# Two feed-forward steps from the middle into self-attention, and a new order of the rest of the middle's steps, in a hosted transformer kernel

## The chip, the cores and the metric

One Trainium2 chip, one core. The metric is the device time of one execution in microseconds; the kernel before has a median of 3263.27 us over 3 runs (3256.77 to 3267.13).

## What is computed

```python
x = xattn0(x, ctx, ctx, 2 * fside)        # 16 heads of 64, 1024 queries, 64 keys, float32; then a layernorm
h1 = ln(x);  x = attn(h1, h1) + x         # self-attention: 16 heads of 32, q, k, v and softmax weights in 8 bits
h2 = ln(x);  x = attn(h2, ctx) + x        # cross-attention: 64 keys, 8 bits
h3 = ln(x)
a, g = split(h3 @ ff_w1 + ff_b1)          # 512 -> 2 x 2048
x = (a * gelu(g)) @ ff_w2 + ff_b2 + x     # 2048 -> 512
```

x has 4 batches of 1024 tokens with 512 features. The projections and the feed-forward are float32 and are computed as three products of high and low parts (hi hi, hi lo, lo hi).

## The kernel before

The 4096 tokens are 8 chunks of 512, two per batch. For each batch the kernel runs `cross` (first attention, layernorm, q, k, v) of both chunks, then for each chunk `self_attention` and `middle` (output projection o1, layernorm h2, q2, cross-attention, o2, layernorm h3). In names such as chunk n, steps have the form kind, group, part: g3.2 is part 2 of group 3.

**The feed-forward of a chunk has no stage of its own.** It is cut into 48 steps, in the order g0 a0 g1 d0 a1 g2 d1 a2 g3 d2 a3 d3, four steps to each. A g step is 128 rows of the gate's half of ff_w1, an a step (the gated rows) 128 rows of the other half, a d step 128 tokens of the product with ff_w2. A step is four quarters of three 128x512 matmuls (L1827, L1828, L1829) into PSUM bank 6 or 7 in turn. The later chunk's stages are the host: at each of their slots every engine calls its own `feed` with the same plan, and that gives the quarters or steps that are due. Behind the matmuls of a g step ScalarE copies the bank with the bias into `gate` (L1283), and after the fourth it runs Gelu over all of `gate` (L1289). Behind an a step VectorE multiplies into `gate` (L1614), ScalarE rounds to u_hi (L1275), GpSimd takes u_lo (L1051). Behind a d step VectorE adds to x (L1537). A d step's matmuls wait for u_lo of its group's last a step. These followers come with a lag in slots: copies, products and additions one slot later, u_hi and u_lo up to two and three slots later in self-attention and one slot later elsewhere.

**Plans** (`host_quarters`, L73). Even chunks use FROM_S: 28 steps in the self-attention of the next chunk and 20 in its middle. Chunks 1, 3 and 5 use FROM_A: 16 steps in the two `cross` stages of the next batch, 18 in the self-attention of its first chunk, 14 in that chunk's middle. Their hosts are chunks 2, 4 and 6. The last chunk stands alone at the end. Within the self-attention the quarters are spread evenly over the 70 slots before the last; in the middle a list of slots says where each step goes.

**Self-attention** has 64 units (head and 128 queries) and 71 slots. In slot s TensorE computes the scores of unit s (L2111, L2112), then the guest's quarters, then the transpose of unit s-5 (L2123), and in half of the slots a part of the weighted values a1 (L2137). VectorE takes the scores out with the row's minimum (L1712) and the transposed weights (L1725), ScalarE takes the exponential (L1353), GpSimd the denominator and the rounding (L1024, L1026, L1031), and once, near slot 10, the bias of o1 (L945). When a head group's a1 is complete, ScalarE's `weighted_high` writes ht_hi (L1224) and the whole back (L1225), and VectorE's `weighted_low` ht_lo (L1439). For the last group both calls stand behind the loop over the slots:

```python
for s in range(S_SLOTS):
    ...
    if n >= 1:
        feed(n - 1, host_plan(n - 1), first_in_S(n) + s)
weighted_high(n, HG - 1)
```

**The middle** has 23 slots. On TensorE, each with the guest's step ahead of it: slots 0 to 3 o1 of four tiles of 128 tokens, 2 to 5 the transposes of h2, 6 to 9 q2, 10 to 13 the scores s2.0 to s2.3 (L2183), 13 to 16 the transposes p2T of the weights (L2191), 14 to 17 the weighted values a2 (L2200), 15 to 18 o2, 19 to 22 the transposes of h3. VectorE does, for each tile of the cross-attention, row maximum, subtraction, row sum and reciprocal (L1761, L1764, L1768 to L1772) and w2T (L1777), GpSimd the scaling and w2b (L1092, L1097). p2T uses one bank, so each transpose waits for w2T of the one before.

**Queues.** SP issues all loads in program order: for a step that is the last user of a piece of ff weights it waits for the step and loads the next piece into the same slot of a ring of three. q2's weights are loaded behind the self-attention's steps, o2's at slot 4 of the middle, the turned queries of the next chunk at slot 12.

Of the kernel before, what the change touches and what calls it, by code (L numbers as in the profile page):

```python
# [72 lines left out]
def host_quarters(in_A, in_S, m_slots):  # L73

    ends = []
    for c in range(NC if in_A else 0):
        for s in range(A_SLOTS):
            ends.append(4 * in_A * c + (4 if s < A_TAIL else (12, 19, 26, 32)[min(s - A_TAIL, 3)]))
    first, start = 4 * NC * in_A, len(ends)
    for s in range(S_SLOTS):  # L80
        ends.append(min(first + 4 * in_S, first + 4 * in_S * (s + 1) // (S_SLOTS - 1)))
    for s in range(M_SLOTS):
        ends.append(first + 4 * in_S + 4 * sum(1 for m in m_slots if m <= s))
    assert ends[-1] == 4 * NF
    return Plan(ends, range(start, start + S_SLOTS))
# [1 line left out]


FROM_S = host_quarters(0, 28, [s for s in range(M_SLOTS) if s not in (16, 21, 22)])
FROM_A = host_quarters(8, 18, (0, 1, 2, 3, 4, 6, 10, 11, 12, 13, 15, 17, 19, 21))  # L90
ALONE = Plan([4 * (k + 1) for k in range(NF)])


def begins_in_A(n):
    return n % NC == NC - 1 and n < CHUNKS - 1


def host_plan(n):
    return FROM_A if begins_in_A(n) else FROM_S

# [163 lines left out]
def build(nc, a, out):  # L264

    ctx = ExitStack()
    with ctx:
# [303 lines left out]
        def _(sp):  # L571
# [139 lines left out]
            def feed(n, plan, i):  # L711

                if n == 0:
                    for v in pieces_due(plan, LAG_KEEP, i):
                        keep_piece(v)
                for k in steps_ending(plan, i):
                    for v in range(PIECES):
                        after = PIECE_NEXT.get((n, v))
                        if PIECE_END[v] == k and after is not None:
                            if not (begins_in_A(after[0]) and after[1] in (0, 8, 9)):  # L720
                                load_piece(*after)
# [50 lines left out]
            def cross(n):  # L772
# [28 lines left out]
                else:  # L801
                    for s in range(A_SLOTS):
                        feed(NC * b - 1, FROM_A, A_SLOTS * c + s)
                if c == 0:
# [85 lines left out]
        def _(pool):  # L890
# [72 lines left out]
            def cross(n):  # L963

                def host(s):
                    if n >= NC:
                        feed(NC * (n // NC) - 1, FROM_A, A_SLOTS * (n % NC) + s)

# [72 lines left out]
            def feed(n, plan, i):  # L1041

                if n == 0:
                    for v in pieces_due(plan, LAG_LOW, i):
                        if v % 2 == 0:
                            piece_low(v)
                for k in steps_due(plan, LAG_LOW, i):
                    kind, j, m = F_STEPS[k]
                    if kind == "a":
                        pool.wait_ge(u_hi_done.sem, u_hi_done.at((n, j, m)))  # L1050
                        pool.tensor_tensor(u_lo[:, m, :], gate[:, m, :], u_hi[:, m, :].bitcast(F32), ALU.subtract  # L1051
                                           ).then_inc(u_lo_done.sem, 1)
# [69 lines left out]
        def _(act):  # L1122
# [141 lines left out]
            def feed(n, plan, i):  # L1264

                if n == 0:
                    for v in pieces_due(plan, LAG_HIGH, i):
                        piece_high(v)
                for k in steps_due(plan, LAG_HIGH, i):
                    kind, j, m = F_STEPS[k]  # L1270
                    if kind == "a":
                        if m == 0 and (j > 0 or n > 0):
                            wait_filled(act, ("f", n if j else n - 1, F_AT["d", j - 1 if j else 3, 3]))
                        wait_emptied(act, ("f", n, k))
                        act.activation(u_hi[:, m, :], gate[:, m, :], ACT.Copy).then_inc(u_hi_done.sem, 1)  # L1275
                for k in steps_due(plan, 1, i):
                    kind, j, m = F_STEPS[k]
                    if kind == "g":
                        key = ("f", n, k)
                        wait_filled(act, key)  # L1280
                        if j > 0 or n > 0:
                            act.wait_ge(u_lo_done.sem, u_lo_done.at((n, j - 1, m) if j else (n - 1, 3, m)))
                        act.activation(gate[:, m, :], bank(bank_of(key)), ACT.Identity,  # L1283
                                       bias=cols["L1_xattn_ff_b1"][:, FT + 4 * j + m:FT + 4 * j + m + 1]
                                       ).then_inc(emptied[bank_of(key)], 1)
                        if m == 3:
                            wait_emptied(act, ("f", n, k - 1))
                            wait_emptied(act, key)
                            act.activation(gate[:], gate[:], ACT.Gelu).then_inc(gelu_done.sem, 1)  # L1289

            def cross(n):

                def host(s):
                    if n >= NC:
                        feed(NC * (n // NC) - 1, FROM_A, A_SLOTS * (n % NC) + s)

# [112 lines left out]
        def _(dve):  # L1409
# [192 lines left out]
            def feed(n, plan, i):  # L1602

                if n == 0:
                    for v in pieces_due(plan, LAG_LOW, i):
                        if v % 2 == 1:
                            piece_low(v)
                for k in steps_due(plan, 1, i):
                    kind, j, m = F_STEPS[k]
                    key = ("f", n, k)  # L1610
                    if kind == "a":
                        dve.wait_ge(gelu_done.sem, gelu_done.at((n, j)))
                        wait_filled(dve, key)
                        emptied_bank(dve.scalar_tensor_tensor(gate[:, m, :], bank(bank_of(key)),  # L1614
                                                              cols["L1_xattn_ff_b1"][:, 4 * j + m:4 * j + m + 1],
                                                              gate[:, m, :], ALU.add, ALU.mult), key)
                    if kind == "d":
                        if j == 0 and m == 0:
                            dve.wait_ge(bias_added.sem, bias_added.at(("ff_b2", n)))
                        residual(key, xs(n, m))  # L1620

            def cross(n):

                def host(s):
                    if n >= NC:
                        feed(NC * (n // NC) - 1, FROM_A, A_SLOTS * (n % NC) + s)

# [180 lines left out]
        def _(pe):  # L1808
# [187 lines left out]
            def feed(n, plan, i):  # L1996

                for quarter in range(plan.ends[i - 1] if i else 0, plan.ends[i]):
                    step_k, k = divmod(quarter, KT)
                    kind, j, m = F_STEPS[step_k]  # L2000
                    key = ("f", n, step_k)
                    o = bank(bank_of(key))
                    if k == 0:
                        wait_empty(key)
                    v = 2 * (step_k // 4)
                    if kind == "d":
                        v += k // 2
                        if m == 0 and k % 2 == 0:
                            wait_piece(pe, n, v)
                        if m == 0 and k == 0:  # L2010
                            pe.wait_ge(u_lo_done.sem, u_lo_done.at((n, j, 3)))
                        r = PIECE_SLOT[n, v]
                        w = [t[r][:].rearrange("p (k n) -> p k n", n=512)[:, k % 2, :] for t in (fw_hi, fw_lo)]
                        ts = slice(m * P, m * P + P)
                        ins = three(o, u_hi[:, k, ts], u_lo[:, k, ts], w[0], w[1], k == 0, k == KT - 1)
                    else:
                        v += m // 2
                        if m % 2 == 0 and k == 0:
                            wait_piece(pe, n, v)
                        if step_k == 0:  # L2020
                            wait_emptied(pe, ("h3T", n, k))
                        r = PIECE_SLOT[n, v]
                        cs = slice(m % 2 * P, m % 2 * P + P)
                        w = [t[r][:].rearrange("p (k n) -> p k n", n=256)[:, k, cs] for t in (fw_hi, fw_lo)]
                        ins = three(o, w[0], w[1], h3_hi[:, k, :], h3_lo[:, k, :], k == 0, k == KT - 1)
                    if k == KT - 1:
                        done(ins, key)
# [8 lines left out]
            def cross(n):  # L2036

                def host(s):
                    if n >= NC:
                        feed(NC * (n // NC) - 1, FROM_A, A_SLOTS * (n % NC) + s)  # L2040

# [210 lines left out]
```

## Time and profile before

| what | us |
|---|---|
| median of 3 runs | 3263.27 |
| the profiled execution, its own time | 3261.57 |
| its span | 3259.8 |
| TensorE busy | 2903.8 (89%) |
| VectorE busy | 2125.2 (65%) |
| ScalarE busy | 1517.4 (47%) |
| GpSimd busy | 1763.0 (54%) |
| mean granted clock of TensorE | 0.94 |
| first to last scores, self-attention of chunks 2, 4, 6 | 131.0, 133.5, 132.9 |
| from there to the next self-attention | 106.9, 106.9, 107.6 |

Times in rows count from the start of the span. PE is TensorE's matmuls, PEld its weight loads, DVE VectorE, ACT ScalarE, POOL GpSimd. A matmul's duration contains its way through the array; matmuls follow each other faster than that. The clock is a share of full speed.

### The profile page before, as it was taken

What the parts mean: (1) busy time and instruction counts of PE and PEld (TensorE: products, weight loads), DVE (VectorE), ACT (ScalarE), POOL (GpSimd) and SP (SyncE); (2) the same over time, 40 slices, a digit from 0 to 9 for tenths busy, and PEclk for the clock granted to TensorE, in tenths of its full rate; (3) what the DMA queues carried; (4) which work ended last, traced back from release to release, by engine and by line L of the source; (5) the groups of instructions that cost most, each with busy time, mean ns of one, the idle gap of its engine ahead of it and who ended that gap; (6) DMA issues with size and microseconds to landing.
All of it is one profiled execution on the core that took longest, in us unless ns stands there. A gap on an engine that the chain in (4) does not pass through costs nothing.

```text
span 3259.8 us, 50933 instructions
## 1 busy us (share of the span) xinstructions
PE 2903.8 (89%) x19712; PEld 2124.7 (65%) x19712; DVE 2125.2 (65%) x3539; ACT 1517.4 (47%) x2258; POOL 1763.0 (54%) x1750
## 2 busy tenths in 40 slices
PE   7677786998799899899899999899989999899998
PEld 6566455566577657667677656666767756666777
DVE  4456686884755596796665497687564588688521
ACT  5343552773333464474333464375333366276321
POOL 3556583883546284585455186386364277377321
PEclk9889657999899999999999999899999989999999
DMA  8754103335443313324443313323453322232444
GB/s 272 246 191 158 59 1 126 133 117 206 150 171 125 118 66 130 136 92 168 147 168 117 126 53 130 128 105 138 147 184 103 149 79 97 92 143 85 174 166 157
DMA packets 199760, 436.42 MB, mean 134 GB/s; under 512 B 94944, under 2 KB 103392, under 8 KB 182368
## 3 DMA queue, kind: packets, MB, share of 16 engines
q1 hardware_dynamic: 199520, 433.15, 37.6%
q8 instruction: 158, 2.59, 0.3%
q14 instruction: 82, 0.67, 0.1%
HBM read 363.38 MB, written 65.54 MB: 132 GB/s over the span
## 4 chain that ended last, share of the span: by engine, by line
PE 59%; POOL 15%; DVE 12%; issue 5%; ACT 5%; DMA 3%; SPq 1%; POOLq 0%; DVEq 0%; ACTq 0%
PE psum L1827 17%; PE psum L1828 16%; PE psum L1829 16%; POOL w1b L1031 6%; PE psum L2123 4%; DVE e L1712 2%; PE psum L2111 2%; POOL rec L1026 2%; PE psum L2137 1%; POOL u_lo L1051 1%; DMA fw_lo<-pieces 1%; DMA unsplit<-in_L_xattn_ff_w 1%; POOL x L945 1%; POOL w_lo L925 1%; DVE w1T L1725 1%
## 5 line engine op out<-in xcount | busy, mean ns | idle before, releaser
L1353 ACT ACTIVATE e<-e,nb 128x1024 f32<-128x1024 f32 x512 | 588.2, 1149 | 331.2 <-DVE e L1712 328.0
L1712 DVE TENSOR_SCALAR_CACHE_REDUCE e<-psum,nscale 128x1024 f32<-128x1024 f32 x512 | 653.0, 1277 | 66.6 <-POOL w1b L1031 44.0
L1031 POOL TENSOR_SCALAR w1b<-e,rec 128x1024 f16<-128x1024 f32 x512 | 578.3, 1130 | 98.5 <-POOL rec L1026 57.3
L1827 PE MATMUL psum<-h_hi,fw_hi 128*128 128x512 f32 x1024 | 460.3, 450 | 44.9 <-DVE h_lo L1439 14.9
L1828 PE MATMUL psum<-h_lo,fw_hi 128*128 128x512 f32 x1024 | 413.4, 404 | 0.0
L1725 DVE TENSOR_SCALAR w1T<-psum 128x1024 bf16<-128x1024 f16 x512 | 352.2, 688 | 93.0 <-PE psum L2123 90.0
L1829 PE MATMUL psum<-h_hi,fw_lo 128*128 128x512 f32 x1024 | 412.4, 403 | 0.0
L2123 PEld LDWEIGHTS psum<-ident,w1b 128*128 128x128 f16 x4096 | 254.2, 103 | 239.9 <-issue 133.9
L2123 PE MATMUL psum<-ident,w1b 128*128 128x128 f16 x4096 | 345.0, 232 | 72.3 <-POOL w1b L1031 40.1
L1827 PEld LDWEIGHTS psum<-h_hi,fw_hi 128*128 128x128 f32 x1024 | 197.5, 193 | 164.8 <-issue 99.6
L1051 POOL TENSOR_TENSOR u_lo<-gate,u_hi 128x512 fp32r<-128x512 f32 x128 | 164.5, 1286 | 225.6 <-ACT u_hi L1275 219.4
L1537 DVE TENSOR_TENSOR x<-psum,x 128x512 f32<-128x512 f32 x192 | 130.7, 685 | 225.6 <-PE psum L1829 225.3
L1827 PE MATMUL psum<-w_hi,ht_hi 128*128 128x512 f32 x640 | 257.5, 402 | 20.1 <-DVE e L1640 13.7
L925 POOL TENSOR_TENSOR w_lo<-mixed,w_hi 128x512 fp32r<-128x512 f32 x140 | 190.1, 1380 | 132.8 <-ACT w_hi L1232 132.8
L1829 PE MATMUL psum<-w_hi,ht_lo 128*128 128x512 f32 x640 | 251.6, 393 | 0.0
L1828 PE MATMUL psum<-w_lo,ht_hi 128*128 128x512 f32 x640 | 251.4, 393 | 0.0
L1827 PE MATMUL psum<-fw_hi,u_hi 128*128 128x512 f32 x512 | 219.7, 429 | 31.5 <-POOL u_lo L1051 14.7
L1024 POOL TENSOR_SCALAR den<-sum,delta 128x2 f32<-128x2 f32 x256 | 75.9, 297 | 285.7 <-ACT e L1353 269.4
L1829 PEld LDWEIGHTS psum<-h_hi,fw_lo 128*128 128x128 f32 x1024 | 199.1, 194 | 46.3
L1170 ACT ACTIVATE qt<-psum,rounder,inv 128x512 f32<-128x512 f32 x128 | 99.9, 780 | 259.1 <-PE psum L1829 256.2
L1828 PEld LDWEIGHTS psum<-h_lo,fw_hi 128*128 128x128 f32 x1024 | 200.0, 195 | 25.3
L2112 PE MATMUL psum<-k_odd,q_turned 32*128 32x512 bf16 x512 | 214.7, 420 | 0.0
(197 smaller groups left out, 6076.1 us busy)
## 6 DMA issues: line engine op xcount, KB each, us to landing
fw_hi<-pieces SPq DMA_DIRECT2D x168, 512.0 KB, 3.3
fw_lo<-pieces SPq DMA_DIRECT2D x168, 512.0 KB, 4.3
w_hi<-kept SPq DMA_DIRECT2D x45, 1024.0 KB, 4.9
w_lo<-kept SPq DMA_DIRECT2D x45, 1024.0 KB, 7.8
mixed<-mixed SPq DMA_DIRECT2D x32, 1024.0 KB, 5.3
fbias<-in_fside_Bx16xSxS SPq DMA_DIRECT2D x64, 256.0 KB, 3.0
unsplit<-in_L_xattn_ff_w SPq DMA_DIRECT2D x24, 512.0 KB, 5.0
pieces<-fw_hi SPq DMA_DIRECT2D x24, 512.0 KB, 2.6
```

What stands on the lines that cost most here:

```text
L925: pool.tensor_tensor(w_lo[s][:, k, :], w_mixed[s][:, k, :], w_hi[s][:, k, :].bitcast(F32), ALU.subtract).then_inc(block_lo_done.sem, 1)
L1031: pool.tensor_scalar(w1b[u % NH][:], e1[u % NE][:], rec1[:, u % 8:u % 8 + 1], HALF, ALU.mult, ALU.add).then_inc(w1_ready.sem, 1)
L1051: pool.tensor_tensor(u_lo[:, m, :], gate[:, m, :], u_hi[:, m, :].bitcast(F32), ALU.subtract).then_inc(u_lo_done.sem, 1)
L1353: act.activation(e1[s % NE][:], e1[s % NE][:], ACT.Exp, bias=nb1[:, s % NE:s % NE + 1], scale=-1.0, accum_out=sum1[:, s % 8:s % 8 + 1]).th ...
L1537: return emptied_bank(dve.tensor_tensor(xt, bank(bank_of(key)), xt, ALU.add), key)
L1712: emptied_bank(dve.tensor_scalar(e1[s % NE][:], psum[:, i:i + 2, :].rearrange("p i n -> p (i n)"), nscale[:, 0:1], LARGEST, ALU.mult, ALU.min,
L1725: emptied_bank(dve.tensor_scalar(w1T[u % 8][:].rearrange("p k q -> p (k q)"), bank(bank_of(key)).bitcast(FP16), -HALF, W_HIGH, ALU.add, AL ...
L1827: pe.matmul(o, s_hi, m_hi, start=first, stop=False)
L1828: pe.matmul(o, s_hi, m_lo, start=False, stop=False)
L1829: return pe.matmul(o, s_lo, m_hi, start=False, stop=last)
L2112: ins = pe.matmul(bank(i + 1), q1_turned[turned, hg, t * P:t * P + P], k1[1][turned, hg, :], start=True, stop=True)
L2123: ins = pe.transpose(bank(bank_of(key)).bitcast(FP16)[:, k * P:k * P + P], w1b[u % NH][:, k * P:k * P + P], ident16[:])
```

## The change

One line, the plan of chunks 1, 3 and 5.

```diff
-FROM_A = host_quarters(8, 18, (0, 1, 2, 3, 4, 6, 10, 11, 12, 13, 15, 17, 19, 21))
+FROM_A = host_quarters(8, 20, (1, 2, 3, 4, 6, 11, 12, 14, 17, 19, 20, 21))
```

The steps' order stays. Self-attention gets steps 16 to 35 instead of 16 to 33, that is g3.2 and g3.3 as well, so 80 quarters instead of 72. The middle's steps by slot:

| | before | after |
|---|---|---|
| g3.2, g3.3 | 0, 1 | (self-attention) |
| d2.0 to d2.3 | 2, 3, 4, 6 | 1, 2, 3, 4 |
| a3.0 to a3.3 | 10, 11, 12, 13 | 6, 11, 12, 14 |
| d3.0 to d3.3 | 15, 17, 19, 21 | 17, 19, 20, 21 |

In self-attention the slots with two quarters are 34 and 69 before, and 6, 13, 20, 27, 34, 41, 48, 55, 62 and 69 after. The copy of a group's fourth g step and its Gelu come one slot behind it: for g3 in slot 2 of the middle before, in slot 70 of self-attention after.

## Rows read from the trace of the kernel before

**Rows 1.** Busy time by stretch: self-attention of chunks 2 and 3, middle of chunk 2.
```profile
core 0: us, PE busy (x) PEld busy (x) DVE busy (x) ACT busy (x) POOL busy (x), PEclk, DMA share, GB/s
1116.10:1247.10 131.00, 119.82 (x1230) 71.31 (x1230) 120.77 (x198) 90.76 (x145) 109.12 (x127) 0.97 0.20 73
1354.00:1496.80 142.80, 140.43 (x1339) 90.72 (x1338) 127.87 (x205) 104.77 (x162) 112.97 (x130) 0.99 0.37 134
...
1247.10:1354.00 106.90, 95.81 (x570) 74.76 (x562) 62.16 (x105) 30.84 (x41) 40.36 (x33) 0.95 0.32 114
```

**Rows 2.** Timeline of TensorE around the softmax of chunk 2's middle.
```profile
start us, us, engine line op out<-in xcount [idle before <-releaser]
1314.67 0.61 PE L2191 MATMUL psum<-ident,w2b 128*128 128x128 f16 x8
1321.43 1.01 PE L2191 MATMUL psum<-ident,w2b 128*128 128x128 f16 x8 [6.15 <-DVE w2T L1777]
...
1325.58 0.76 PE L1827 MATMUL psum<-fw_hi,u_hi 128*128 128x512 f32 x1 [2.58 <-POOL u_lo L1051]
...
1330.44 0.62 PE L2191 MATMUL psum<-ident,w2b 128*128 128x128 f16 x8
```

**Rows 3.** The same view, slot 10: q2.3's last matmul, a3.0's first, s2.0.
```profile
1299.77 0.39 PE L1829 MATMUL psum<-ht_hi,w_lo 128*128 128x512 f32 x1
1299.99 0.39 PE L1827 MATMUL psum<-h_hi,fw_hi 128*128 128x512 f32 x1
...
1302.71 0.61 PE L2183 MATMUL psum<-k,q2T 128*128 128x256 bf16 x4
```

**Rows 4.** Busy time by stretch: slots 21 to 63 of chunks 2 and 3.
```profile
1161.50:1247.40 85.90, 80.34 (x899) 48.69 (x898) 82.73 (x136) 63.16 (x101) 72.92 (x88) 1.00 0.17 63
1402.90:1497.30 94.40, 94.33 (x970) 61.52 (x969) 85.40 (x138) 67.14 (x105) 76.43 (x91) 1.00 0.26 91
```

**Rows 5.** The same for L1827 alone, one matmul to a quarter.
```profile
core 0: us, PE busy (x) PEld busy (x), PEclk, DMA share, GB/s
1161.50:1247.40 85.90, 20.88 (x42) 7.82 (x42) 1.00 0.17 63
1402.90:1497.30 94.40, 30.12 (x66) 12.29 (x66) 1.00 0.26 91
```

**Rows 6.** Two gaps of TensorE (timeline), and busy time by stretch behind their starts.
```profile
1143.75 1.04 PE L2123 MATMUL psum<-ident,w1b 128*128 128x128 f16 x8 [4.34 <-POOL w1b L1031]
...
1142.20:1149.10 6.90, 5.35 (x55) 3.33 (x55) 3.88 (x6) 3.00 (x5) 6.00 (x8) 0.51 0.00 0
...
789.25 0.79 PE L1827 MATMUL psum<-h_hi,fw_hi 128*128 128x512 f32 x1 [4.84 <-ACT gate L1283]
...
787.30:794.10 6.80, 4.85 (x11) 3.80 (x12) 1.95 (x3) 2.88 (x4) 0.00 (x0) 0.50 0.38 154
```

**Rows 7.** Timeline of ScalarE, end of chunk 2's self-attention and slots 1 and 2.
```profile
1258.62 0.69 ACT L1283 ACTIVATE gate<-psum,col_L_xattn_ff_b 128x512 f32<-128x512 f32 x1 [4.74 <-PE psum L1829]
1259.21 0.68 ACT L1224 ACTIVATE ht_hi<-psum,unit_v 128x512 fp32r<-128x512 f32 x1
...
1267.59 0.69 ACT L1283 ACTIVATE gate<-psum,col_L_xattn_ff_b 128x512 f32<-128x512 f32 x1 [4.75 <-PE psum L1829]
1268.35 1.28 ACT L1289 ACT_TABLE_LOAD   x1
1269.64 1.92 ACT L1289 ACTIVATE gate<-gate 128x2048 f32<-128x2048 f32 x1
```

**Rows 8.** Timeline of VectorE in the same place.
```profile
1260.47 0.69 DVE L1439 TENSOR_TENSOR ht_lo<-psum,ht_hi 128x512 fp32r<-128x512 f32 x1 [2.60 <-ACT psum L1225]
```

**Rows 9.** Timeline of TensorE in the same place: last of a1, first of o1.
```profile
1258.52 0.63 PE L2137 MATMUL psum<-w1T,v 128*32 128x128 bf16 x32
...
1261.94 0.39 PE L1827 MATMUL psum<-w_hi,ht_hi 128*128 128x512 f32 x1
```

**Rows 10.** Timeline of TensorE, s2.0 of chunk 0, which hosts nothing.
```profile
533.17 0.60 PE L2183 MATMUL psum<-k,q2T 128*128 128x256 bf16 x4 [1.71 <-issue]
```

**Rows 11.** Timeline of VectorE in chunk 2's softmax.
```profile
1321.20 0.73 DVE L1614 SCALAR_TENSOR_TENSOR gate<-psum,col_L_xattn_ff_b,gate 128x512 f32<-128x512 f32 x1
...
1324.32 0.63 DVE L1777 TENSOR_SCALAR w2T<-psum 128x1024 bf16<-128x1024 f16 x1
```

**Rows 12.** Timeline of GpSimd in chunk 2's softmax.
```profile
1323.04 1.05 POOL L1097 TENSOR_SCALAR w2b<-e 128x1024 f16<-128x1024 f32 x1 [0.22 <-POOL e L1092]
1324.17 1.27 POOL L1051 TENSOR_TENSOR u_lo<-gate,u_hi 128x512 fp32r<-128x512 f32 x1
```

## The prediction

> **What bounds the kernel now.** I read first the table of stages. In self-attention that hosts an odd chunk (chunk 2's) VectorE is busy for 120.8 of 131.0 us; where it hosts an even one (chunk 3's, 28 steps) TensorE is, 140.4 of 142.8 [rows 1]. So the first has room on TensorE. The middle is TensorE's: 95.8 of 106.9 us [rows 1]. Then I read what TensorE waits for inside chunk 2's middle; it repeats in the middles of chunks 4 and 6, so each price below counts three times. It has one hole, in the softmax of the cross-attention: behind the first transpose it idles 6.15 us for VectorE, and a little later 2.58 us for u_lo of a3.3 [rows 2].
>
> **Part 1: two steps, g3.2 and g3.3, go into self-attention.** A step is 12 matmuls, a quarter 3 of them. At full clock they follow each other by 0.227 us (12 from 1299.99 to 1302.71 [rows 3]), so a quarter is 0.68 us, a step 2.72. The plan gives one quarter to each of the 70 slots and a second where it rounds up: before in slots 34 and 69, now in 6, 13, 20 and so on to 69, eight more. The moved steps bring VectorE nothing, ScalarE two 0.69 us gate copies and Gelu.
>
> What does a quarter cost there? From slot 21 to 63 the two kinds of stage show 85.9 us with 42 quarters and 94.4 us with 66 [rows 4, 5]: 0.35 us per quarter along that line. TensorE is saturated at its upper end (94.3 of 94.4), VectorE nearly at its lower (82.7 of 85.9), so the first quarters are cheaper: I take 0.25 for the five that fall there, 1.2 us. The three before slot 21 meet a stage that is filling or at half clock (after the 4.34 us for which TensorE waits for GpSimd, busy with the bias, the clock is at 0.51 for 6.9 us [rows 6]); I take 0.8. Sum **+2.0**; bounds 0 (all in TensorE's slack) and 8 x 0.68 = 5.4. The gate copies hide in ScalarE's idle time, 40 of 131 us. SP's loads of the pieces move up with their steps; each piece has the slot of a ring of three and a step now takes 131/20 = 6.6 us against 7.3, so no load gets late. GpSimd's and VectorE's work of a1, d1 and a2 keeps its count and comes earlier.
>
> **Part 2: the end of self-attention.** Here I see the main cost. g3.1 ends the stage's quarters now; its copy runs at 1258.62, and right behind it on ScalarE comes ht_hi of the last head group at 1259.21 [rows 7]. From there VectorE's ht_lo starts 1.26 us later, at 1260.47 [rows 8], and o1's first product follows, at 1261.94, hidden behind g3.2 (TensorE ends a1 at about 1258.9 and is busy all along [rows 9]). With the change g3.3 is the step whose copy stands there, and `feed` adds the whole gate's Gelu behind it, in slot 70, ahead of `weighted_high(n, 3)`, which stands after the loop. From the start of that copy to the end of Gelu it is 3.97 us in the old place: 1267.59, a table load of 1.28, Gelu of 1.92 until 1271.56 [rows 7]. So Gelu ends at 1258.62 + 3.97 = 1262.6, ht_hi follows, ht_lo starts 1.26 later and ends 0.69 later: 1264.5, and o1 starts at 1264.6. Nothing covers it, since slot 0 of the middle is now empty. Against 1261.94 that is **+2.7**, with g3.2's 2.72 us of matmuls already gone from in front of o1. Bounds: -0.6 if ht_hi were not delayed (ht_lo ends 1261.16 now), +3.3 if o1's handover were slow.
>
> The Trainium skill, page "ScalarE: Activation LUTs", section "What ACT_TABLE_LOAD costs", puts a switch of sets at 1283 ns and 1380 ns of drain. The load agrees; this trace shows no drain (0.08 us idle before the load, Gelu 0.01 after it [rows 7]). By the page the term would be 4.1 instead of 2.7, an estimate.
>
> **Part 3: the clock behind that gap.** TensorE would stand from 1258.9 to 1264.6, 5.7 us. The nearest rows: 4.34 us of idle time, then 6.9 us at 0.51; 4.84 us, then 6.8 us at 0.50 [rows 6]. Both are the level of 1.2 GHz, and begin 3.3 us into the gap. Taken over: half clock from 1262.2 to 1269.1, of which 4.5 us hold work, half of it lost: **+2.2** (bounds 0 and 3.4).
>
> **Part 4: slots 1 to 10 of the middle.** d2.0 to d2.3 each take the place of another step, and a3.0 goes from slot 10 to slot 6, where d2.3 was. There its gate product and its u_hi lie ahead of the quantisations of q2.1, in idle time of VectorE and ScalarE, and u_lo in GpSimd's. Slot 10 loses 2.72 us, but q2's last rounding, which a3.0 covered, is bare: in chunk 0, with no guest, s2.0 waits 1.71 us [rows 10]. q2.3's last matmul, at 1299.77 for 0.39, then gives s2.0 at 1301.9 instead of 1302.71 [rows 3]: **-0.9** (bounds 0 and -2.7).
>
> **Part 5: the softmax hole.** From s2.0 on VectorE has no gap; the pace of s2.1 and s2.2 is the same, since a3.1 and a3.2 stay. a3.3 goes from slot 13 to 14, behind the first transpose, and fills part of the 6.15 us. Its gate product (0.73, at 1321.20) leaves the chain ahead of the last sum, so w2T.1 ends at about 1324.3 instead of 1324.95 [rows 11]. d3.0, which waits for u_lo of 1324.17 + 1.27 = 1325.44, moves from slot 15 to 17, and the third transpose, w2b being ready at 1324.09, can go at 1324.45 instead of TensorE's standing until 1325.58 [rows 2, 12]: **-1.1** (bounds 0 and -2.0). What follows to the end of the middle is the same list of products in another order, dense before, and three steps behind o2.3 instead of two cover its norm. Half clock cost d3.0 4.86 us instead of 2.72 here (1325.58 to 1330.44 [rows 2]), 2.1 too much. Two or three gaps of under 4 us take the place of the long one; I count **-0.5** (bounds -2.1 and +2.1). If that cover is gone, o2's products are what half clock hits.
>
> Sum for one pair: 2.0 + 2.7 + 2.2 - 0.9 - 1.1 - 0.5 = 4.4 us; three times 13.2. The profiled execution took 3261.57 us (span 3259.8, 1.8 around it) and comes to 3274.8; the median of the three runs is 1.7 above it, so I forecast 3276.5.
>
> **Rivals.** A measurement of this kernel can tell about 0.3%, 9.8 us, from no change.
>
> *Wash.* Self-attention takes the quarters at nothing, and TensorE stays at full clock over the new gap: 0 + 2.7 + 0 - 0.9 - 1.1 - 0.5 = 0.2 a pair, 3264. For it: VectorE's 92% in [rows 1]. Against: both gaps in [rows 6] were shorter and brought half clock. With one of the two terms alone it is 3270 to 3271, still within 0.3%. Chance 0.36.
>
> *Faster: the clock.* The mechanism is half clock that goes away: a fuller self-attention keeps TensorE at full clock behind GpSimd's bias (6.9 us at 0.51 [rows 6], 3.4 us back), and the refilled hole does the same for o2 (2.1). With the quarters free and the new gap at full clock: -3.4 + 2.7 - 0.9 - 1.1 - 2.1 = -4.8 a pair, 3249. It decides if GpSimd's bias no longer starves TensorE for over 4 us; against it, that wait is for w1b, which more quarters don't bring earlier. Chance 0.10.
>
> *Slower still: quarters at full price.* Each second quarter of a slot stalls VectorE and is never regained, 5.4 instead of 2.0, and half clock stays through the broken hole: 5.4 + 2.7 + 3.4 - 0.9 - 1.1 + 1.5 = 11.0 a pair, 3296. For it: the line through [rows 4, 5] is already half of the full price. Chance 0.10.
>
> *The switch with a drain.* If ScalarE needed some more time between the copy and the load, 1.4 us as a bound, that is 4.2 us in all, 3281. The copy and the load stand 0.07 us apart [rows 7]. The drain of the page named above, in the Trainium skill, would be such a time. Chance 0.04.
>
> *The change doesn't do what it says.* The plan is read in the code: quarters 64 to 143 in the 70 slots, so this has no chance worth a number.
>
> The forecast case has 0.40. Range: from 3256, two thirds of the way from no change to the faster rival, to 3289, where the terms' upper bounds begin to add up. Faster 0.10, same 0.36, slower 0.54 (0.40 + 0.10 + 0.04).
>
> **What would show it.** In the profile after, at the end of self-attention of chunks 2, 4 and 6: a table load and Gelu directly ahead of ht_hi, ht_lo 3.3 us later against a1's end, and o1's first product after 5 to 6 us of idle time with VectorE's ht_lo as releaser, then half clock. The self-attention itself 133 us instead of 131. s2.0 released by q2T. The hole in pieces of 4, 4 and under 2 us, d3.0 behind o2.1. I am wrong if ht_hi does not stand behind Gelu, if the clock holds over the gap, or if the stage from slot 21 to 63 grows by over 3 us or not at all.

## The result and the profile after

The changed kernel takes 3281.83 us (median of 5 runs, 3278.30 to 3287.16) against 3264.19 (5 runs): ratio 1.0057, 95% interval 1.0045 to 1.0069. It is 0.57% slower; 17.6 us lie between the medians, 13.2 were forecast. Executions in a slower state are left out of every ratio here and below, and the one trace of `e2_cover` is of such an execution and is not read.

The profiled execution has a span of 3283.0 us, 23.2 more than before. To see where, I cut each trace at the same instructions: the first scores of each self-attention, its last scores, the last matmul of a1, the first of o1, the first scores s2.0 of the cross-attention and the first matmul of the third transpose p2T.2 (L2191). Start to start, in us, for the three chunks that host an odd one. A pair is such a chunk's self-attention and middle together; half clock means a granted clock of 0.50, the level of 1.2 GHz.

| from, to | before: chunks 2, 4, 6 | after: chunks 2, 4, 6 | mean change | forecast |
|---|---|---|---|---|
| first to last scores | 131.0, 133.6, 132.9 | 134.6, 138.0, 134.8 | +3.3 | +2.0 |
| to the end of a1 | 11.8, 11.8, 12.1 | 12.3, 12.3, 12.3 | +0.4 | 0 |
| to o1 | 3.02, 3.04, 3.04 | 5.77, 5.77, 5.78 | +2.7 | +2.7 |
| to s2.0 | 40.8, 40.7, 40.7 | 42.9, 42.6, 41.4 | +1.5 | +1.3 (2.2 - 0.9) |
| to p2T.2 | 27.7, 27.7, 28.1 | 21.4, 21.4, 21.4 | -6.4 | |
| to the next self-attention | 23.6, 23.6, 23.6 | 27.8, 29.2, 28.5 | +4.9 | -1.6 with the row above |
| the whole pair | 237.9, 240.4, 240.5 | 244.8, 249.3, 244.2 | +6.5 | +4.4 |

d3.0 has changed sides of the cut at p2T.2, so those two rows go together: -1.5. Three pairs make 19.5 us, close to the 17.6 of the medians. The other 3.7 us of this profile are what is left of larger differences in stages that the change leaves alone: 4.5 us more ahead of chunk 0's first scores, 3.9 more from there to chunk 1's (221.7 before, 225.6 after), 1.6 more from there to chunk 2's, and 5.6 less from chunk 5's first scores to chunk 6's (513.3 before, 507.6 after). More on this at the end.

The end of chunk 2's self-attention, ScalarE, timeline after; it answers to [rows 7]:

```profile
start us, us, engine line op out<-in xcount [idle before <-releaser]
1272.72 0.69 ACT L1283 ACTIVATE gate<-psum,col_L_xattn_ff_b 128x512 f32<-128x512 f32 x1 [4.73 <-PE psum L1829]
1273.48 1.28 ACT L1289 ACT_TABLE_LOAD   x1
1274.78 1.91 ACT L1289 ACTIVATE gate<-gate 128x2048 f32<-128x2048 f32 x1
1276.59 0.67 ACT L1224 ACTIVATE ht_hi<-psum,unit_v 128x512 fp32r<-128x512 f32 x1
```

VectorE and TensorE in the same place, answering to [rows 8, 9]:

```profile
1277.85 0.69 DVE L1439 TENSOR_TENSOR ht_lo<-psum,ht_hi 128x512 fp32r<-128x512 f32 x1 [5.88 <-ACT psum L1225]
...
1272.61 0.63 PE L2137 MATMUL psum<-w1T,v 128*32 128x128 bf16 x32
1278.80 0.77 PE L1827 MATMUL psum<-w_hi,ht_hi 128*128 128x512 f32 x1 [5.55 <-DVE ht_lo L1439]
```

Gelu stands between the copy and ht_hi, 3.97 us from the start of the copy to its end as in its old place, and o1 waits 5.55 us for ht_lo, behind the chain copy, table load, Gelu, ht_hi. Busy time by stretch after; the clock is the last column but two:

```profile
core 0: us, PE busy (x) PEld busy (x) DVE busy (x) ACT busy (x) POOL busy (x), PEclk, DMA share, GB/s
1278.10:1285.00 6.90, 6.20 (x15) 4.94 (x16) 1.07 (x2) 0.00 (x0) 0.00 (x0) 0.51 0.63 252
...
1126.20:1260.70 134.50, 126.00 (x1254) 76.71 (x1254) 121.66 (x199) 91.88 (x148) 109.61 (x128) 0.96 0.21 79
1260.70:1370.90 110.20, 93.27 (x546) 72.72 (x538) 61.53 (x104) 29.26 (x39) 40.42 (x32) 0.94 0.28 101
...
1173.00:1262.00 89.00, 85.18 (x917) 52.83 (x915) 83.71 (x138) 63.87 (x101) 72.94 (x89) 0.98 0.20 72
```

The gap is followed by 6.9 us at half clock. The two stages answer to [rows 1]. The last row is slots 21 to 63, 89.0 us where [rows 4] have 85.9; VectorE is idle for 5.3 us of it instead of 3.2.

The softmax of chunk 2's middle, TensorE, timeline after, answering to [rows 2, 10]:

```profile
1321.69 0.60 PE L2183 MATMUL psum<-k,q2T 128*128 128x256 bf16 x4 [1.71 <-issue]
...
1333.09 1.03 PE L2191 MATMUL psum<-ident,w2b 128*128 128x128 f16 x8 [3.94 <-POOL w2b L1097]
1333.88 0.78 PE L1827 MATMUL psum<-h_hi,fw_hi 128*128 128x512 f32 x1
...
1340.39 0.61 PE L2191 MATMUL psum<-ident,w2b 128*128 128x128 f16 x8 [2.46 <-DVE w2T L1777]
...
1343.10 1.03 PE L2191 MATMUL psum<-ident,w2b 128*128 128x128 f16 x8 [1.76 <-POOL w2b L1097]
1344.07 0.64 PE L2200 MATMUL psum<-w2T,v 128*64 128x128 bf16 x8
1344.63 0.80 PE L1827 MATMUL psum<-w_hi,ht_hi 128*128 128x512 f32 x1
```

s2.0 waits the 1.71 us of [rows 10] to the hundredth. The one hole is now three idle times of 3.94, 2.46 and 1.76 us with a3.3 in between, and p2T.2 goes 21.4 us behind s2.0.

What I had not priced is in the middle of self-attention, where g2's Gelu stands in slot 28. ScalarE, GpSimd, VectorE and TensorE behind it, timelines after:

```profile
1190.01 1.28 ACT L1289 ACT_TABLE_LOAD   x1
1191.30 1.92 ACT L1289 ACTIVATE gate<-gate 128x2048 f32<-128x2048 f32 x1
1193.24 1.28 ACT L1353 ACT_TABLE_LOAD   x1
1194.53 1.15 ACT L1353 ACTIVATE e<-e,nb 128x1024 f32<-128x1024 f32 x1
...
1195.87 0.29 POOL L1024 TENSOR_SCALAR den<-sum,delta 128x2 f32<-128x2 f32 x1 [3.41 <-ACT e L1353]
...
1198.41 1.28 DVE L1712 TENSOR_SCALAR_CACHE_REDUCE e<-psum,nscale 128x1024 f32<-128x1024 f32 x1 [1.74 <-POOL w1b L1031]
1203.29 0.69 DVE L1725 TENSOR_SCALAR w1T<-psum 128x1024 bf16<-128x1024 f16 x1 [1.78 <-PE psum L2123]
...
1198.35 0.62 PE L2123 MATMUL psum<-ident,w1b 128*128 128x128 f16 x8 [1.90 <-POOL w1b L1031]
1199.56 0.75 PE L1827 MATMUL psum<-fw_hi,u_hi 128*128 128x512 f32 x1
...
1199.60:1203.00 3.40, 3.40 (x15) 2.50 (x14) 1.91 (x5) 2.48 (x4) 3.00 (x4) 0.50 0.00 0
```

While ScalarE has Gelu in place of exponentials, GpSimd runs dry for 3.41 us, VectorE for 1.74, TensorE for 1.90. Then the clock is at half for 3.4 us, and in it lie the six matmuls of slot 34, one of those with two quarters: VectorE waits again, 1.78 us. In the kernel before, with this Gelu in slot 32, the same three waits are 2.60, 1.05 and 1.21 us, and the clock holds.

Cut at VectorE's first instruction of slots 21, 42 and 63, slots 21 to 41 take 43.9 to 44.1 us before and 45.9 after, slots 42 to 62 take 42.0 and 43.1. How much of the first is the clock can be read from `e7_high_cover`, a run below that has the same quarters in self-attention as the changed kernel. Its slots 21 to 41 in chunks 2 and 6, where only the first has half clock behind Gelu:

```profile
1175.50:1221.40 45.90, 43.28 (x458) 26.80 (x457) 41.68 (x69) 34.11 (x53) 35.87 (x45) 0.96 0.14 48
2670.30:2714.60 44.30, 41.65 (x458) 25.83 (x458) 41.65 (x70) 34.06 (x52) 35.54 (x45) 1.00 0.15 51
```

VectorE's first wait is 1.74 us in both. So at full clock the two more quarters of these slots cost 0.2 us, and the half clock costs 1.6. Of the 12 such stages in the traces of the changed kernel, `e1_high_first`, `e3_move_only` and `e7_high_cover`, 11 have that half clock and take 45.8 or 45.9 us.

### The profile page after: what moved, and what is told of

It is laid out like the page before. It is cut to its first block, busy times and chain, and to the rows that moved or that the text cites. A ratio compares the mean times of both kernels' runs of the same rounds, so it can differ in the third digit from the quotient of the medians.

```text
span 3283.0 us, 50933 instructions
## 1 busy us (share of the span) xinstructions
PE 2915.3 (89%) x19712; PEld 2136.9 (65%) x19712; DVE 2122.1 (65%) x3539; ACT 1517.3 (46%) x2258; POOL 1759.0 (54%) x1750
## 4 chain that ended last, share of the span: by engine, by line
PE 61%; DVE 12%; POOL 11%; issue 5%; ACT 5%; DMA 3%; SPq 1%; POOLq 0%; DVEq 0%; ACTq 0%
PE psum L1827 18%; PE psum L1828 16%; PE psum L1829 16%; PE psum L2123 5%; POOL w1b L1031 4%; PE psum L2111 3%; DVE e L1712 3%; PE psum L2137 2%; POOL rec L1026 1%; DMA unsplit<-in_L_xattn_ff_w 1%; DVE w1T L1725 1%; POOL x L945 1%; DMA fw_lo<-pieces 1%; POOL w_lo L925 1%; DVE e L1764 1%
## 5 line engine op out<-in xcount | busy, mean ns | idle before, releaser
L1827 PE MATMUL psum<-h_hi,fw_hi 128*128 128x512 f32 x1024 | 461.1, 450 | 41.5 <-DVE h_lo L1439 14.9
L1827 PEld LDWEIGHTS psum<-h_hi,fw_hi 128*128 128x128 f32 x1024 | 197.8, 193 | 160.0 <-issue 98.7
L1827 PE MATMUL psum<-w_hi,ht_hi 128*128 128x512 f32 x640 | 263.5, 412 | 36.8 <-DVE ht_lo L1439 19.2
L1537 DVE TENSOR_TENSOR x<-psum,x 128x512 f32<-128x512 f32 x192 | 130.9, 686 | 243.2 <-PE psum L1829 243.2
L1827 PE MATMUL psum<-fw_hi,u_hi 128*128 128x512 f32 x512 | 218.4, 427 | 22.1 <-POOL u_lo L1051 7.0
```

Source lines behind the costliest of these rows:

```text
L1537: return emptied_bank(dve.tensor_tensor(xt, bank(bank_of(key)), xt, ALU.add), key)
L1827: pe.matmul(o, s_hi, m_hi, start=first, stop=False)
```

## The experiments

Theory A is the prediction's: Gelu ahead of ht_hi holds up o1, and half clock follows. Rival B: the quarters in self-attention are the cost. Rival C: the new order of the middle is a loss of its own. The runs of a group below were compared with the kernel before on the same chip, which had medians of 3263.03, 3263.32 and 3264.20 us in the three groups. Stage times are from each run's trace, cut as above.

**ht_hi ahead of Gelu** (`e1_high_first`), on the changed kernel:

```diff
+                    if s == S_SLOTS - 1:
+                        weighted_high(n, HG - 1)
                     if n >= 1:
                         feed(n - 1, host_plan(n - 1), first_in_S(n) + s)
-                weighted_high(n, HG - 1)
```

> The changed kernel with one difference: in the last slot of self-attention ScalarE writes ht_hi of the last head group before the guest's gate copy and Gelu, not behind them. Theory A (Gelu ahead of ht_hi holds up o1, and the gap brings half clock): TensorE's gap ahead of o1 falls from 5.77 us to about 2.5, the half clock behind it (3.4 to 6.8 us) goes; 3.3 + about 2.5 us for each of three pairs, so about 3264 us instead of 3281.8. Rival B (the eight more quarters in self-attention are what costs, the gap is hidden by something later): not more than 4 us come back, 3278 or above.

Measured: 3269.05 us, ratio 1.0015 (1.0004 to 1.0026). Timelines of ScalarE and TensorE in this run (from L1363 on lines are one higher):

```profile
1265.78 0.69 ACT L1224 ACTIVATE ht_hi<-psum,unit_v 128x512 fp32r<-128x512 f32 x1 [5.28 <-PE psum L2138]
1266.36 0.65 ACT L1225 ACTIVATE psum<-psum,unit_v 128x512 f32<-128x512 f32 x1
1266.93 0.69 ACT L1283 ACTIVATE gate<-psum,col_L_xattn_ff_b 128x512 f32<-128x512 f32 x1
1267.69 1.28 ACT L1289 ACT_TABLE_LOAD   x1
...
1268.00 0.47 PE L1828 MATMUL psum<-w_hi,ht_hi 128*128 128x512 f32 x1 [2.27 <-DVE ht_lo L1440]
```

From a1's last matmul to o1's first it is 2.49 us in all three chunks, 2.27 of it idle, no half clock follows, and from o1 to s2.0 it is 40.0 us each time. The pairs take 240.1, 240.1 and 239.9: 6.1 less than the changed kernel's mean. That two calls of ScalarE in another order bring back some 13 of the 17.6 us shows theory A, though the total stays 5 us above the 3264 that I expected. By stage the cure is worth 3.3 us ahead of o1 and 2.3 behind it, and 0.6 of that is lost again between s2.0 and the next self-attention: 5.0 a pair. The other 1.1 of the 6.1 lie in self-attention, which the edit does not touch: in the changed kernel's profile chunk 4 has 13.7 us of half clock near its start, and 138.0 us where the other two have 134.6 and 134.8. In this run the self-attention keeps its 134.7. The edit acts in the odd chunks too; their stretches show no shift that all traces with it share.

**d2.0 in slot 0** (`e2_cover`), on the changed kernel:

```diff
-FROM_A = host_quarters(8, 20, (1, 2, 3, 4, 6, 11, 12, 14, 17, 19, 20, 21))
+FROM_A = host_quarters(8, 20, (0, 2, 3, 4, 6, 11, 12, 14, 17, 19, 20, 21))
```

> The changed kernel with d2.0 in slot 0 of the middle instead of slot 1, so that its matmuls stand in the gap ahead of o1. Theory A: o1 starts when it did (ht_lo sets it), the gap is 2.7 us of matmuls and about 3.1 us idle, and slot 1 loses a step: 2.7 us and perhaps 1.5 to 3 us of half clock for each pair, 3265 to 3270 us. Rival B (the middle's length is set elsewhere, by the softmax of the cross-attention): under 3 us in all, 3279 or above.

Measured: 3265.17 us, ratio 1.0012 (1.0001 to 1.0023), as theory A has it, at the lower end of its range. Only its times are used: that o1 still starts when it did, with Gelu ahead of ht_hi, and how much half clock is left, was not seen. What d2.0 in slot 0 does by stage can be read only together with the other cure, in `e7_high_cover` below.

**The quarters moved, the middle's order old** (`e3_move_only`), on the changed kernel:

```diff
-FROM_A = host_quarters(8, 20, (1, 2, 3, 4, 6, 11, 12, 14, 17, 19, 20, 21))
+FROM_A = host_quarters(8, 20, (2, 3, 4, 6, 10, 11, 12, 13, 15, 17, 19, 21))
```

> 20 steps in self-attention as in the changed kernel, but the middle's twelve steps in their old slots (2, 3, 4, 6, 10 to 13, 15, 17, 19, 21). Theory A says the new order is a gain of 0.9 (slot 10), 1.5 (softmax) and 0.6 us (behind it) for each pair, so this is 9 us slower than the changed kernel, about 3291. Rival C (the new order of the middle is itself a loss): it is faster than the changed kernel, 3275 or below.

Measured: 3276.76 us, ratio 1.0038 (1.0025 to 1.0051), between the two, but 5 us below the changed kernel, where 9 above were forecast. My 3291 was a fault of reckoning: I counted the 0.9 us of slot 10 as a gain of the order. It is the sum of a step that leaves (-2.7, in this run too) and of the bare rounding of q2 (+1.9), and only the second belongs to the order. So the order's share is +1.9 in slot 10 against -1.5 in softmax and behind: about nothing. From o1 to the next self-attention this run takes 91.7, 92.0 and 91.7 us, the changed kernel 92.1, 93.2 and 91.3; of the 1.8 us a pair by which this run's profile is shorter, 1.4 lie in self-attention, where the plan is the same.

**The order alone** (`e4_order_only`), 18 steps in self-attention:

```diff
-FROM_A = host_quarters(8, 18, (0, 1, 2, 3, 4, 6, 10, 11, 12, 13, 15, 17, 19, 21))
+FROM_A = host_quarters(8, 18, (0, 0, 1, 2, 3, 4, 6, 11, 12, 14, 17, 19, 20, 21))
```

> 18 steps in self-attention as before; the middle has g3.2 and g3.3 both in slot 0 and the other twelve in the changed kernel's slots. Theory A: Gelu comes in slot 1, behind ht_hi, no gap ahead of o1; the middle gains 1.5 + 0.6 in the softmax and loses 1.8 where q2's rounding is bare: 0 to -1 us for each pair, 3261 to 3265 us. Rival C (the new order is a loss): above 3270.

Measured: 3264.28 us, ratio 1.0006 (0.9998 to 1.0015); pairs of 237.8, 240.1 and 237.9 us, 1.0 below before on the mean. Rival C falls: the order as a whole costs nothing that can be seen here, and brings nothing either. Self-attention is 130.9, 132.8 and 131.1 here and 134.3, 134.5 and 134.3 in the run above: the eight quarters cost 2.8 us there and 0.6 in the tail to a1's end (12.3 against 11.7), and the order has no part in it.

**The second quarters away from Gelu** (`e5_doubles_away`), on the changed kernel. `host_quarters` takes a list of the slots with two quarters:

```diff
+        if doubles:
+            ends.append(min(first + 4 * in_S, first + s + 1 + sum(1 for d in doubles if d <= s)))
...
-FROM_A = host_quarters(8, 20, (1, 2, 3, 4, 6, 11, 12, 14, 17, 19, 20, 21))
+FROM_A = host_quarters(8, 20, (1, 2, 3, 4, 6, 11, 12, 14, 17, 19, 20, 21),
+                       doubles=(6, 9, 13, 20, 38, 45, 48, 55, 62, 69))
```

> The changed kernel with the slots of two quarters at 6, 9, 13, 20, 38, 45, 48, 55, 62, 69: Gelu of g2 stays in slot 28 of self-attention, but slots 27 and 34 next to it have one quarter. Theory D (a second quarter right ahead of and behind Gelu is what stalls VectorE: 1.74 and 1.78 us of idle time in slots 32 and 34, and 3.4 us of half clock): slots 21 to 41 take about 44 us instead of 46.0, self-attention of chunks 2 and 6 132.5 instead of 134.7, about 3275 us in all. Rival E (each more quarter costs its share of TensorE's time wherever it stands): 134.5 as before, 3280.

Measured: 3280.62 us (4 executions), ratio 1.0053 (1.0039 to 1.0067), not told from the changed kernel, and by the total what rival E has. The stage speaks for theory D only in part. Between the first instructions of VectorE in slots 21 and 42, chunk 2 takes 44.7 us and chunks 4 and 6 43.5, the changed kernel 45.9, and self-attention of chunks 4 and 6 is 132.2 and 132.3. But chunk 2's is 135.3, with 10.2 us of half clock in its first slots and 3.4 behind Gelu, where chunks 4 and 6 have neither. So what moving the two quarters changed is the second stall (under 0.8 us now) and, in two chunks of three, the half clock; the whole gained too little to show. The first stall behind Gelu stays what it was, so the quarters beside it are not its cause; VectorE, chunk 6 (in this run and the next, lines behind the plan are four higher):

```profile
2696.18 1.28 DVE L1716 TENSOR_SCALAR_CACHE_REDUCE e<-psum,nscale 128x1024 f32<-128x1024 f32 x1 [1.81 <-POOL w1b L1035]
```

**Gelu in slot 29** (`e6_gelu_slot_29`), one entry of that list moved:

```diff
-                       doubles=(6, 9, 13, 20, 38, 45, 48, 55, 62, 69))
+                       doubles=(6, 13, 20, 38, 45, 48, 52, 55, 62, 69))
```

> As the run with doubles away, with one double moved from slot 9 to slot 52, so that Gelu of g2 comes in slot 29. GpSimd takes units in pairs and waits for the odd one's exponential, so behind slot 29 it has a pair left to work on while ScalarE is away. Theory F (this pairing matters): VectorE's idle time behind Gelu falls under 1.5 us and the stage is 1 us shorter than with doubles away, 3272. Rival: the same within 0.5 us a stage, 3275.

Measured: 3271.47 us, ratio 1.0024 (1.0012 to 1.0036), the total of theory F. VectorE behind Gelu, chunk 2:

```profile
1197.49 1.28 DVE L1716 TENSOR_SCALAR_CACHE_REDUCE e<-psum,nscale 128x1024 f32<-128x1024 f32 x1 [1.12 <-POOL w1b L1035]
```

The stall is 1.12 us instead of 1.81; slots 21 to 41 take 42.7 us in each of the three chunks, and no half clock follows Gelu in any of them. With slots 42 to 62 (43.0) that makes 85.7 us with six slots of two quarters; the changed kernel has 89.0 with as many, the kernel before 86.1 with one. So there the five more quarters of slots 21 to 62 cost nothing, in these slots and with this Gelu. The stage as a whole is not 1 us shorter, as theory F has it: first to last scores are 133.6, 133.5 and 131.8 us, 133.0 on the mean against 133.3 with doubles away, since slots 0 to 20 of chunks 2 and 4 have 10.2 us of half clock at their start. The rest of the gain is in the tail behind the last scores, 11.6 instead of 12.3, and 0.9 a pair behind o1's start, which no theory had named. That the pairing of units in `scale_unit` shortens the stall fits the trace but was not varied by itself; the kernel before has a stall of 1.05 us with Gelu in slot 32, an even slot like 28, so the pairing alone does not say where it is short.

**Both cures of the gap** (`e7_high_cover`): the edits of `e1_high_first` and `e2_cover` together.

> The changed kernel with both cures: ht_hi ahead of Gelu, and d2.0 in slot 0 of the middle. Theory A: no gap ahead of o1 (3.0 us from a1's last matmul to o1's first, as before), 40.0 - 2.7 = 37.3 us from there to the scores of the cross-attention, so 2.2 us for each pair below the run with ht_hi first: 3262 us, level with the kernel before, because what is left is self-attention's 2 to 3 us. Rival: the gap of 2.5 us that it closes was hidden, 3268.

Measured: 3259.65 us, ratio 0.9988 (0.9979 to 0.9997). From a1 to o1 it is 3.02 to 3.04 us, from there to s2.0 37.2, a pair 237.1 on the mean, 2.9 below `e1_high_first`. With 20 steps in self-attention the kernel is now level with the one before or slightly faster, so the loss of the move goes with an end of self-attention that fits it. It is no gain yet: the next run gets as far with the middle's order alone.

**Only the softmax's order** (`e8_softmax_order`), on the kernel before:

```diff
-FROM_A = host_quarters(8, 18, (0, 1, 2, 3, 4, 6, 10, 11, 12, 13, 15, 17, 19, 21))
+FROM_A = host_quarters(8, 18, (0, 1, 2, 3, 4, 6, 10, 11, 12, 14, 17, 19, 20, 21))
```

> The kernel before (18 steps in self-attention, 14 in the middle) with only a3.3 moved from slot 13 to 14 and d3.0 to d3.3 from 15, 17, 19, 21 to 17, 19, 20, 21. Theory A: the softmax gains 1.5 us and what follows it 0.6, and a3.0 still covers q2's rounding in slot 10, so 2.1 us for each pair: about 3257 us. Rival C (the new order gives nothing, since half clock comes back in the broken hole): 3263.

Measured: 3260.19 us, ratio 0.9984 (0.9975 to 0.9993), pairs of 237.1, 236.7 and 239.2, 1.9 below before on the mean. So this half of the change is a gain by itself, but of less than I gave it, and less than the pairs say: from s2.0 to the next self-attention, the only part that the edit touches, it is 1.05 us shorter on the mean (50.4 against 51.5) where 2.1 were forecast. The other 0.9 lie in self-attention and its tail. Half clock did come back in the broken hole, as rival C has it: 13.7, 13.7 and 10.2 us in the three chunks against 10.2 each before. But the gains are 1.0, 1.1 and 1.1 us, so its return is not seen to have cost anything. TensorE in chunk 2's softmax:

```profile
1316.98 1.03 PE L2191 MATMUL psum<-ident,w2b 128*128 128x128 f16 x8 [3.66 <-POOL w2b L1097]
...
1324.30 0.61 PE L2191 MATMUL psum<-ident,w2b 128*128 128x128 f16 x8 [1.42 <-DVE w2T L1777]
...
1327.01 1.03 PE L2191 MATMUL psum<-ident,w2b 128*128 128x128 f16 x8 [1.76 <-POOL w2b L1097]
```

**All three** (`e9_all_three`): `e7_high_cover` with the quarters of `e6_gelu_slot_29`.

> The run with both cures of the gap (ht_hi ahead of Gelu, d2.0 in slot 0) with the quarters of the run that has Gelu in slot 29 (second quarters in 6, 13, 20, 38, 45, 48, 52, 55, 62, 69). If the three findings add up, a pair takes 237.1 us less 1.7 in self-attention (134.6 to about 133.0) and 0.7 in its tail (12.3 to 11.6), 234.7 us: 7 us below the run with both cures, about 3253 us, and 0.3% below the kernel before. If they don't (the stage before only shifts work into half clock), 3259.

Measured: 3253.38 us, ratio 0.9972 (0.9955 to 0.9988). Busy time by stretch, the two stages of chunk 2:

```profile
1116.60:1248.80 132.20, 125.57 (x1256) 76.22 (x1256) 121.77 (x199) 92.28 (x148) 110.66 (x128) 0.96 0.21 80
1248.80:1350.60 101.80, 91.28 (x544) 71.15 (x540) 61.61 (x105) 28.75 (x39) 39.81 (x32) 0.95 0.30 109
```

The pairs take 234.0, 236.1 and 234.0, 234.7 on the mean, which was forecast: the findings add up. (The profiled execution, at 3244.98 us, was one of the shortest; the forecast is compared with the median.)

**Second quarters in the tail** (`e10_tail_doubles`): there, slots 55 and 62 for 65 and 67.

> As the run with all three, but the second quarters of slots 55 and 62 moved to 65 and 67, behind the last scores, where TensorE idles 0.5 to 1.0 us in each slot. Theory G (TensorE's idle time of the tail takes them): self-attention 1 us shorter, tail longer by under 0.5, 0.5 us a pair, 3251. Rival: the tail is a chain through GpSimd and TensorE and grows by the 1.4 us that they cost, 3254.

Measured: 3253.09 us, ratio 0.9968 (0.9956 to 0.9981), level with the last, though the traced pairs are 1.0 us longer on the mean. The tail grows from 11.7 to 13.0 us, by what the two quarters cost, as the rival has it; self-attention is 132.3 instead of 132.7. Theory G falls. Its premise does not hold either: in the trace of `e9_all_three` TensorE is busy for 11.2 of the tail's 11.7 us, so the idle time that was to take the quarters is 0.5 us in all and not in each slot.

## Why the prediction was right, and where it was off

- **Direction and size.** Slower, 17.6 us where 13.2 were forecast, inside the range. The largest term of the forecast, part 2, came as worked out: 2.74 us a pair for 2.7, the gap 5.77 for 5.7, with the releasers named.
- **Part 3, half clock: the mechanism is right, the size is in part luck.** In `e1_high_first`, which has none behind its gap, o1 to s2.0 takes 40.0 us; the changed kernel takes 42.9, 42.6 and 41.4, that is 2.9, 2.6 and 1.4 too much, 2.3 on the mean for 2.2. But the clock fell 5.1, 4.5 and 5.2 us behind the start of a1's last matmul, not 3.3, so more of the half clock reached work (6.2 and 5.6 us where 4.5 were worked out), and in the third chunk it lasted only 3.4 us instead of 6.8, of which 2.8 reached work. The two errors cancel in the mean. What holds in each chunk is that about half of the time at half clock in which TensorE has work is lost. The same gap of 5.77 us stands in `e3_move_only`, `e5_doubles_away` and `e6_gelu_slot_29`: half clock followed in all nine chunks, and cost 1.7 to 3.0 us (for `e3_move_only` against before's 40.7 less a step of 2.7).
- **Part 4.** 40.0 against the 40.7 to 40.8 before: -0.7 for -0.9 (by its own numbers the prediction's difference is 0.84). The waiting time of chunk 0 carried over exactly.
- **Part 5.** -1.5 for -1.1 and -0.5 together, but -2.1, -0.6 and -1.8 in the three chunks. The same order gives -0.9 in `e1_high_first`, -1.8 in `e4_order_only` and, all but a3.0, -1.05 in `e8_softmax_order`. So the agreement to 0.1 us is partly luck too.
- **Part 1 was sized too low, by a term that it put at nothing.** Self-attention and its tail grew by 3.7 us in the profile (3.4 between `e4_order_only` and `e3_move_only`), not 2.0. The price of the quarters, read from a line between two kinds of stage [rows 4, 5], was about right: 1.1 us for the three of slots 42 to 62 and, where the clock holds, 0.2 for the two of slots 21 to 41, where 1.2 were forecast for all five. What was left out is g2's Gelu, which moved from slot 32 to 28. Behind it VectorE waits 1.74 us instead of 1.05, TensorE 1.90 instead of 1.21, and 3.4 us of half clock follow where there was none: 1.6 us in every chunk but one of the four kernels with these quarters. By the window of [rows 4] slots 21 to 63 grew by 3.1 us, which by my own list is a little over the bound of being right there. The tail's 0.4 us had no term either. In `e6_gelu_slot_29` as many quarters in these slots cost nothing. Why the wait is longer with Gelu in slot 28 than in slot 32 stays open, and so does why half clock follows it in 11 of 12 stages with a second quarter on either side and in one of three without (`e5_doubles_away`).
- **The range.** Its lower end, 3256, is half of the way from 3263 to the faster rival's 3249 and not two thirds, which would be 3254. Nothing hangs on it here.
- **The rivals.** Of the wash, the half with the quarters at nothing is refuted by `e3_move_only` against `e4_order_only` (2.8 us), the half with full clock over the gap by the trace. The faster rival's mechanism came in a small part: behind GpSimd's bias TensorE's matmuls still start 3.0 to 4.4 us apart in all three chunks, but half clock lasts 3.4, 6.8 and 3.4 us there instead of 6.8 each time. Self-attention did not get shorter by it. Of the slowest rival, quarters at full price, 5.4 us, part 1 reached 3.7, and the hole's half clock did not grow. The rival of a switch with a drain named 3281, which is the measured time to 1 us; that is chance. The table load begins 0.07 us behind the copy here too, and Gelu 0.02 us behind the load, so there was no such time. The Trainium skill, "ScalarE: Activation LUTs", "What ACT_TABLE_LOAD costs", gives 1283 ns of load and 1380 ns of drain for a switch. The trace agrees with the load (1.28 us) and shows no drain in this place.

## What to carry to other kernels

When background work is moved between stages, look first at which instructions of the other engines come with it, and behind what they then stand in an in-order queue: here the 24 matmuls that moved cost self-attention 3.4 to 3.7 us a pair, nearly half of it half clock behind another Gelu, and one Gelu ahead of one short copy cost 5.0. At a handover between two stages keep a filler for TensorE and put the copy that the next stage waits for ahead of everything that can wait. And a rate taken from a whole stage prices the work, not what it does to a stall: shifting a stall by a few slots made it 0.7 us longer and brought half clock behind it, which cost more than the quarters did.

## What I had not expected of the hardware

Half clock followed the same gap for 6.8 us in two chunks and 3.4 in the third. It also followed an idle time of 1.90 us behind g2's Gelu, in all three chunks. And the profiled executions differ where the kernels do not. The stretch from chunk 0's first scores to chunk 1's, the same instructions in every kernel, took 221.7 to 222.2 us in five of the traces (before, `e1_high_first`, `e5_doubles_away`, `e8_softmax_order`, `e9_all_three`) and 225.5 to 225.7 in six others, nothing between. Most of the difference lies in chunk 0's middle, in the part from o1 to s2.0 (36.5 to 36.9 us with 6.8 us of half clock, or 38.9 to 39.0 with 10.2) and in the last one (19.2 to 19.4 or 21.0 to 21.1). Other stretches that no plan here changes differ as much: 349.2 to 354.8 us ahead of chunk 0's first scores, 505.7 to 513.3 from chunk 5's first scores to chunk 6's, 404.3 to 410.4 from chunk 7's to the end. That is as much as some of the terms here, so single profiles of this kernel were compared stage by stage and totals by their intervals. What decides between the lengths was not tried.
